# Row maxima of attention blocks: the transpose of the folded maxima as a DMA within SBUF in place of two TensorE transposes

## The reference

```python
qh = _split_heads(jnp.einsum('bnq,qi->bni', x, Wq))          # 8 heads, 1792 x 128
kh = _split_heads(jnp.einsum('bmc,ci->bmi', context, Wk))    # 8 heads, 6000 x 128
vh = _split_heads(jnp.einsum('bmc,ci->bmi', context, Wv))
sim = jnp.einsum('hid,hjd->hij', qh, kh) * SCALE
mean = jnp.mean(sim, axis=-1, keepdims=True)
sim = (sim - mean) * ATTN_MATRIX_SCALE + mean                # a shift of a row: softmax keeps only the 1.5
attn = jax.nn.softmax(sim, axis=-1)
out = jnp.einsum('hij,hjd->hid', attn, vh)
```

## Time and profile before

| | |
|---|---|
| median of 3 runs | 2304.46 us (2302.53 to 2307.41) |
| the profiled execution, its own time | 2306.85 us |
| its span in the profile | 2305.1 us |
| mean granted clock of TensorE | 0.996 of full speed |
| PE busy | 2252.5 us (98%) |
| DVE busy | 2020.4 us (88%) |
| POOL busy | 1898.6 us (82%) |
| ACT busy | 1865.1 us (81%) |
| first and last reduction to row maxima (L1095) | at 193.1 and 2173.9 us |
| DMA | 50.44 MB, mean 22 GB/s |

### The profile page before, as it was taken

How to read it: one execution, slowest core, us unless ns; L and a number is a source line. 1 busy time by engine, 2 the same in 40 slices (tenths; PEclk the granted TensorE clock), 3 DMA queues, 4 the chain that set the end, 5 groups by cost and what they waited for, 6 DMA issues and landing times.

```text
span 2305.1 us, 61948 instructions
## 1 busy us (share of the span) xinstructions
PE 2252.5 (98%) x26078; PEld 1980.7 (86%) x26078; DVE 2020.4 (88%) x2241; ACT 1865.1 (81%) x2224; POOL 1898.6 (82%) x1153
## 2 busy tenths in 40 slices
PE   7998999999999999999999999999999999999998
PEld 4557998899889998899888998899889998998886
DVE  7878988988889888988898898988899888898876
ACT  4357888888888888888878888888888888888855
POOL 8675888888878888888888898888878888899953
PEclk8999999999999999999999999999999999999999
DMA  7400000000000000000000000000000000010220
GB/s 201 158 32 21 6 4 13 4 7 6 11 6 4 7 13 4 6 4 7 13 4 5 6 13 4 6 4 7 13 4 6 4 6 6 4 47 7 90 79 33
DMA packets 34837, 50.44 MB, mean 22 GB/s; under 512 B 2304, under 2 KB 27392, under 8 KB 34560
## 3 DMA queue, kind: packets, MB, share of 16 engines
q1 hardware_dynamic: 34560, 46.46, 6.5%
HBM read 30.99 MB, written 15.47 MB: 20 GB/s over the span
## 4 chain that ended last, share of the span: by engine, by line
PE 71%; POOL 15%; DVE 6%; issue 4%; ACT 3%; POOLq 0%; DVEq 0%; ACTq 0%
PE psum L420 26%; POOL e_lo L1618 12%; PE psum L452 9%; PE psum L445 9%; PE psum L450 5%; PE psum L448 5%; PE psum L567 4%; PE psum L557 4%; POOL e_hi L1612 3%; DVE run_max L1082 3%; ACT ring L847 2%; PE psum L693 2%; PE psum L740 1%; PE psum L529 1%; PE psum L574 1%
## 5 line engine op out<-in xcount | busy, mean ns | idle before, releaser
L1618 POOL TENSOR_TENSOR e_lo<-ring,e_hi 128x1024 f16<-128x1024 f32 (+1 forms) x665 | 1388.8, 2103 | 196.4 <-ACT ring L862 160.8
L1082 DVE TENSOR_TENSOR run_max<-psum,run_max 128x1024 f16<-128x1024 f32 (+1 forms) x616 | 737.9, 1198 | 183.5 <-ACT ring L847 180.3
L847 ACT ACTIVATE ring<-psum 128x1024 f32<-128x1024 f32 (+1 forms) x672 | 673.7, 1003 | 180.0 <-PE psum L420 104.8
L1103 DVE SCALAR_TENSOR_TENSOR ring<-ring,psum 128x1024 f32<-128x1024 f32 (+1 forms) x672 | 792.5, 1186 | 0.7 <-PE psum L660 0.7
L420 PE MATMUL psum<-qx_hi,k_hi 128*128 128x256 f16 x2632 | 718.0, 273 | 15.5 <-DVE run_max L1082 9.1
L420 PE MATMUL psum<-qx_hi,k_lo 128*128 128x256 f16 x2632 | 717.8, 273 | 0.0
L420 PE MATMUL psum<-qx_lo,k_hi 128*128 128x256 f16 x2632 | 717.7, 273 | 0.0
L452 PE MATMUL psum<-v_main,e_lo 128*128 128x129 f16 x4032 | 711.4, 220 | 0.0
L862 ACT ACTIVATE ring<-ring 128x1024 f32<-128x1024 f32 (+1 forms) x672 | 696.1, 1036 | 1.3 <-DVE ring L1103 0.7
L445 PE MATMUL psum<-v_main,e_hi 128*128 128x257 f16 x2016 | 550.4, 273 | 1.3 <-POOL e_lo L1618 1.3
L450 PE MATMUL psum<-v_main,e_hi 128*128 128x128 f16 x2016 | 446.9, 222 | 0.0
(11 more groups left out here) (203 smaller groups left out, 3171.2 us busy)
## 6 DMA issues: line engine op xcount, KB each, us to landing
o_scratch<-o_buf SPq DMA_DIRECT2D x56, 128.0 KB, 1.9
raw<-o_scratch SPq DMA_DIRECT2D x14, 512.0 KB, 4.4
stage<-in_ctxT SPq DMA_DIRECT2D x6, 500.0 KB, 3.9
stage<-in_ctxT SPq DMA_DIRECT2D x12, 250.0 KB, 4.9
w_scratch<-wall SPq DMA_DIRECT2D x1, 2304.0 KB, 10.9
wall<-w_scratch SPq DMA_DIRECT2D x6, 384.0 KB, 3.2
x<-in_xT SPq DMA_DIRECT2D x4, 448.0 KB, 6.6
res<-in_x SPq DMA_DIRECT2D x1, 1792.0 KB, 17.6
```

Source lines behind the costliest of these rows:

```text
L847: a.activation(ring[:, f % SLOTS, 0:n], pair(f)[:, 0:n], ACT.Copy).then_inc(s_kept, 1)
L1082: ins = v.tensor_tensor(run_max[:, 0:n], pair(f)[:, 0:n], run_max[:, 0:n], ALU.max)
L1103: v.scalar_tensor_tensor(slot, slot, LIFT, psum[:, 6, 0:QB].unsqueeze(1).broadcast_to([P, t, QB]), ALU.add, ALU.subtract).then_inc(s_sub, 1)
L1618: g.tensor_tensor(e_lo[f % NEL][:, 0:n], slot, e_hi[f % NEH][:, 0:n], ALU.subtract).then_inc(s_lo, 1)
```

## The change

The two PE transposes of each block and their task in the side bank are taken out. SP issues one DMA transpose per block instead, from `fold` to a new SBUF tile `fold_t` (128 x 2 x 128 fp16, 64 KB, on the place of self-attention statistics that are no longer used). DVE's `rows_max` reads `fold_t`, at the same place of its queue, after the DMA's count `s_turned`; PE's `spread` waits for `s_row`. `fold_max` now also waits until the transpose of the block before has landed, and `rows_max` until PE has spread the block before.

```diff
+        fold_t = at(15104, "fold_t", [P, QT, P], F16)
...
-        side16 = psum[:, 7, 0:QB // 2].bitcast(F16)
+        s_turned, s_row = sem("b_turned"), sem("b_row")
...
-            if s == MAX_S + 2:
-                return ("t", 0, h) if n + 1 < NBLK else None
...
-                def transposes(n_at, number):
-                    pe.wait_ge(s_fold, n_at + 2)
-                    pe.wait_ge(s_free, number)
-                    for t in range(QT):
-                        mm = pe.transpose(side16[:, t * P:(t + 1) * P], fold[:, t * P:(t + 1) * P], ident16[:, :])
-                    mm.then_inc(s_side, 1)
-
-                def spread(n, n_at, number):
-
-                    pe.wait_ge(s_free, number + 1)
+                def spread(n, n_at):
+
+                    pe.wait_ge(s_row, n_at + 2)
                     if n >= 0:
                         pe.wait_ge(s_sub, n_at * NGRP + NGRP)
...
                 def fold_max(n):
                     v.wait_ge(s_max, n * NGRP + NGRP)
+                    if n > 0:
+                        v.wait_ge(s_turned, n * 16)
...
-                def rows_max(number):
-                    v.wait_ge(s_side, number + 1)
-                    v.tensor_reduce(row_max[:, :], side16.rearrange("p (t k) -> p t k", t=QT), AX.X,
-                                    ALU.max).then_inc(s_free, 1)
+                def rows_max(n):
+                    v.wait_ge(s_turned, n * 16 + 16)
+                    if n > 0:
+                        v.wait_ge(s_bc, n)
+                    v.tensor_reduce(row_max[:, :], fold_t[:, :, :], AX.X, ALU.max).then_inc(s_row, 1)
...
+                def turn(n):
+
+                    sp.wait_ge(s_fold, n + 1)
+                    if n > 0:
+                        sp.wait_ge(s_row, n)
+                    sp.dma_start_transpose(fold_t[:, :, :], fold[:, :]).then_inc(s_turned, 16)
...
+                turn(0)
+                turn(1)
                 for n in range(NBLK):
                     h, qb = n // NQB, n % NQB
                     store(h, qb)
+                    if n + 2 < NBLK - 1:
+                        turn(n + 2)
...
                         for i in range(3):
                             load_tile(i)
+                        turn(NBLK - 1)
                         sp.wait_ge(s_qk, NF_ALL)
```

More of the change, by code:

```diff
@@ L753, in step @@
                     task = side_of(n, s)
-                    if task is not None:
-                        if task[0] == "t":
-                            transposes(n_at, number)
-                        elif not behind(n, s):
-                            side(n, s, past, number)
+                    if task is not None and not behind(n, s):
+                        side(n, s, past, number)
                     if n >= 0:
@@ L766, in step @@
                     if s == MAX_S + 2 and -1 <= n < NBLK - 1:
-                        spread(n, n_at, number)
+                        spread(n, n_at)
                     turn = n * NGRP + s - TAIL
@@ L1008, in _ @@
                     task = side_of(n, s)
-                    if task is not None and task[0] != "t" and not behind(n, s):
+                    if task is not None and not behind(n, s):
                         high_half(n, s, number)
@@ L1405, in _ @@
                 v.memset(v_tail[:, :, DH:OW], 1.0).then_inc(s_init, 1)
-                number, halves = 0, 0
+                halves = 0
                 for f, n, s in steps():
@@ L1415, in _ @@
                     task = side_of(n, s)
-                    if task is not None and task[0] == "t":
-                        rows_max(number)
+                    if s == MAX_S + 2 and -1 <= n < NBLK - 1:
+                        rows_max(n + 1)
                     if f + LEAD < NF_ALL:
@@ L1422, in _ @@
                     if task is not None:
-                        if task[0] != "t":
-                            halves += 1
-                            low_half(n, s, halves)
-                        number += 1
+                        halves += 1
+                        low_half(n, s, halves)
                     if s == 2 and n > 0:
```

## The result

The changed kernel took 2315.35 us (median of 6 runs, 2313.35 to 2318.08) against 2305.95 us for the kernel before in runs beside it. The ratio is 1.0037, with a 95% interval from 1.0027 to 1.0047: slower by 8.5 us, 6.2 to 10.8; the two medians as they stand are 9.4 us apart. The forecast was 25 us slower. The profiled execution took 2314.5 us, its span is 2312.7 us, 7.6 us over the span before.

A forecast was written before the change was run, and what follows sets the result against it. PE was taken to bound the kernel. With a 2.9 us transfer, roomy blocks gave -3.2 us, tight ones +26.3, the last +1.9: +25.0, so 2329.5 us; 8-in-10 range 2303 to 2402, the forecast's own 2309 to 2336.

The forecast's parts named there:

- PE as the bound: Claim that PE, busy 98% of the span, sets the time in every part the change touches.
- the offset: Per block, end of DVE's fold to start of PE's spread: 3.81 us roomy, 2.46 tight before; new forecast 3.47.
- where the loss falls: 26 tight blocks lose 1.01 us each, the last block 1.9; 29 roomy blocks gain 0.11 each.
- tight blocks: 26 blocks where DVE folds later against PE, which arrives 0.1 us before the maxima; +26.3 us forecast.
- roomy ones: 29 blocks where PE reaches the spread after the maxima and does not wait; -3.2 us forecast.
- T: Time from issue to landing of the DMA transpose, taken as 2.9 us, between ends of 1.9 and 4.4.
- the slow case: Rival: the transfer is slow and PE waits in every block; +102.3 us at a 4.4 us landing, chance 0.30.
- The faster case: Rival: landing in 1.6 us or less gains the PE transposes and PE's waits for the reduction; -9.2 us, chance 0.06.
- DVE does not catch up ... I count nothing: DVE idles 1.1 us per tight block and stays late; nothing counted for ACT and POOL shrinking PE's idle time.
- The signs: Expected in the profile: landing 2.2 to 3.1 us, DVE waits about 1.1 in tight blocks, PE's spread wait near 29.
- The reduction from SBUF: DVE's row-maxima reduction, reading SBUF instead of PSUM, taken at the old 0.41 us, with bounds 0.29 and 2.11.
- The other queues: Stores and loads queued around the transposes cost nothing; one still running would delay one transpose a few microseconds, once.

The follow-up runs named there:

- no DMA: The changed kernel without its DMA, DVE reducing `fold` itself in place: 2303.41 us against 2307.19 for the kernel before, ratio 0.998.
- twice the transfer: The changed kernel with the transpose made twice, the second waiting for the first: 2451.51 us against 2307.24 for the kernel before, ratio 1.0632.

## Why the prediction was right and wrong

- **PE as the bound, the offset, and where the loss falls**: right. Waits grew in tight blocks and in the last, roomy ones gained 0.11 each where the transfer was in time, and without the wait the loss was gone (no DMA: 0.998). SP's wake is 0.03 us as taken, and DVE starts 0.02 after the landing, so T + 0.05 and not T + 0.1: 2.32 us from fold to reduction, with T 2.28 when it is taken to two places. The spread follows the reduction by 0.06 us in some heads and 0.13 in others; the prediction reads 0.13 from its own row and adds 0.06.
- **T**: this is the step that failed, "I take T = 2.9, one microsecond over the nearest row". It is 2.3, 0.4 over that row. In the prediction's own sum T = 2.3 gives an offset of 2.87: 26 x 0.41 - 3.2 + 1.3 = +8.8 us, and 8.5 was measured. That it comes so close is in part luck. In the profiles the tight blocks grew by 8.1 and not 10.7 us (4.3 were given back by other waits), and the roomy ones shrank by 1.0 and not 3.2 (late transfers); the two misses cancel. The form was wrong as well: I expected the regrouping of data to cost more the more there is, but half of it lands in 2.2 us. The 0.5 us over a plain copy lie behind the start of the data, mostly in how late the last packets, of 4 bytes, come; why they come so late no run shows. The other end, 4.4, was taken from a transfer of eight times the bytes and made the slow case heavier than it deserved.
- **The rule on a transpose's price** in the Trainium skill (VectorE: DVE Perf Modes, "The three transpose paths"), 1309 ns per 128 x 128 by DMA, taken in series for T = 2.6: from issue to landing one of 128 x 128 took 2.2 us here, and the second costs 0.1 more, not 1.3. The advice of the same page of the Trainium skill ("Rules for kernel authors"), TensorE where PSUM will do, was right for this kernel as it stood. **The rule that a transpose is as fast as a regular DMA** in the Trainium skill (Advanced Engine Details and Errata, "X-Bar Transpose (TRN2)") does not hold here at 64 KB from issue to landing: 2.3 against 1.8 us for the same bytes.
- **"The faster case", -9.2 us**: wrong. PE's waits at the spread in the kernel before came from DVE's 1.92 us of own work between fold and reduction, not from the transposes, so a faster way through could not take them. Without any transfer the gain was 4.6 us.
- **"DVE does not catch up ... I count nothing"**: nearly right. 4.3 us of the 15.2 in tight blocks were given back, mostly by K products that no longer waited for `k_lo`; at twice the transfer it was 6.7 of 70.5.
- **The signs**: the landing (2.3 us, inside 2.2 to 3.1) and PE's waits (22.5 us in 30 blocks, for "near 29 us" in 26) came. DVE waited 0.3 to 0.4 us in tight blocks and not 1.1, as T was shorter. It waited for the DMA in the roomy ones too, 0.17 us in most: the 2.66 us counted there as DVE's own work hold the 0.50 that it waited for the transposes, which the change took away. That cost nothing.
- **The reduction from SBUF** stayed at 0.42 us, as taken; the stretch to 2.11 did not come.
- **The clock** is a term that the prediction did not have. It mattered little here, one stretch at 1.2 GHz in either kernel behind the first spread, but 29 us at twice the transfer.
- **The other queues** cost nothing but for one thing that I had left out: in nine of the 56 blocks the reduction came 2.6 us or more after the fold, below.

## What to carry to other kernels

When a step's result moves to a DMA, set its latency (from issue to landing, here 2.3 us for a transpose of 64 KB, 2.2 for one of 32 KB and 1.8 for a copy of 64 KB) against the work that the waiting engines have in between, block by block: the mean slack hides that half of the blocks have none. Look first for an engine that does fixed work between producer and consumer (DVE's 1.92 us): a transfer faster than that buys nothing more, and most of what is slower is paid for. And a wait removed in blocks where two engines are nearly level comes back under another name, so measure the block's length and not the wait. When stands of PE of 3 us are added, look at the granted clock behind them before other waits are blamed.

## What was unexpected of the hardware

Issuing a transposing DMA holds SP's queue for 1.17 us, where a plain copy of the same tile holds it for 0.47 and the store of twice the bytes for 0.36. Yet the data of transpose and copy start at nearly the same time, 1.17 and 1.13 us after the issue begins.

Transfers within SBUF come late when instructions are loaded beside them. Two windows of 5 us around one transpose each, in the changed kernel (queue q8 carries instructions; then the issue and us to landing):

```profile
q1 hardware_dynamic: 288, 0.07, 7.0%
q8 instruction: 1, 0.02, 1.9%
...
fold_t<-fold SPq DMA_TRANSPOSE x1, 4.0
...
q1 hardware_dynamic: 288, 0.07, 6.6%
...
fold_t<-fold SPq DMA_TRANSPOSE x1, 2.3
```

The first has one 16 KB packet of the instruction queue in flight and lands in 4.0 us, the second has none and lands in 2.3. Each of the nine transfers with 2.6 us or more from fold to reduction had a packet of an instruction queue in flight in that time; of the 33 transfers without one none was late, and 14 with one were on time. Over the eight kernels with such a DMA none of 309 transfers without an instruction packet was more than 0.2 us over its kernel's median; of 195 with one 77 were. The delay goes with the packet: in eight of the nine it had 16 KB and ended 1.1 to 2.8 us after the issue, and the data landed 1.0 to 1.6 us after that; where a 16 KB packet ended within 0.9 us of the issue the transfer was on time. In the run with plain copies (up to 3.5 us) seven were late, and in all seven 15 of the DMA's 16 semaphore counts came in time, within 1.83 us, and the last one alone was late. That looks like one of the 16 DMA engines being busy with instructions. No run here took the instruction loads away, so the cause is argued, closely, and not shown. The late ones account for up to the 2.4 us of new waits in the roomy blocks.

A DVE reduction over a strided fp16 tile in SBUF took 1.93 to 1.99 us for 1,024 elements per partition in every block, while the pair of two-input instructions on the same data took 1.4 to 3.3 us behind the first block. The second of the pair took 0.29 us in the first block, with POOL idle beside it, 1.0 in 41 blocks with POOL's cast (L1612) beside it for most of the time, and 2.1 in 14 with POOL's two-input instruction (L1618) beside it. No run changed POOL's work alone.
